# Expert weights loaded once into the first halves of two attention buffers, their row statistics taken on ScalarE, and the last retention units reordered

## Chip, core and metric

The kernel runs on one core of a Trainium2 chip. TensorE (PE) multiplies matrices, VectorE (DVE) and ScalarE (ACT) work on tiles of 128 partitions, GpSimd (POOL) does small arithmetic and indirect DMAs, SyncE (SP) issues most DMAs. The metric is the device time of one execution in microseconds (us). The profile is one such execution taken by the hardware profiler. The granted clock of TensorE stands in it as a share of 2.4 GHz: 1.00 is 2.4 GHz, 0.50 is 1.2 GHz.

## What is computed

The input x holds four sequences of 512 tokens with 128 channels. Four blocks are added to it, one after another: two retention layers with a feed-forward part and a final layer norm, a mixture of experts, causal attention, and the same mixture of experts again. Cut to its core:

```
x = x + retention_layers(layernorm(x))    # 2 layers, 16 heads, decay; FFN 128->512->128 with gelu; ends in layernorm(.., lnf_g, lnf_b)
x = x + moe(layernorm(x))                 # below
x = x + attention(layernorm(x))           # causal, 16 heads of 8, + bo
x = x + moe(layernorm(x))

def moe(x):                               # 2048 tokens, 8 experts, the best 2 of each token
    w, i = top_k(softmax(x @ gate_w), 2); w = w / w.sum(-1)
    return sum over experts e of  (silu(x @ w1[e]) * (x @ w3[e])) @ w2[e]  * (weight of e)
```

The expert weights w1 and w3 are 8 x 2 matrices of 128 x 512 in float32. The kernel multiplies with them as a sum of two float16 parts, high and low, scaled by a power of two for each expert; for the scale it needs a bound on the largest weight of the expert.

## The kernel before

The program has one instruction stream for each engine, written by hand; semaphores tie them together, and every engine takes its stream in order. It has four stages: `blocks()` (the retention layers), `experts(0)`, `attention()`, `experts(1)`.

`blocks()` runs over 8 units (n; two layers times four sequences) of four token tiles each, thus 32 steps t = 4n + u, and two more steps to drain. In step t PE does `keys_values(t)` (L1872), `scores(t)` (L1883), `project_out(t-2)` (L1919), `retain(t-1)` (L1900, L1905, L1909), and, by the position u in the unit, two of the feed-forward's up projections of unit n-2 (L1925; u = 0, 1), the queries and keys of the next unit (L1808; u = 2), or the down projection (L1934) and the transposition for the next feed-forward (`plain_turn(*ln_up(n-1))`, L1797; u = 3). DVE opens each step with the addition of the key and value bias (L985), then multiplies the scores with the decay (L1000, twice), adds outputs, and gates (L1011). ACT copies what PE leaves in the two ring banks of PSUM and does the activations; which use of the banks follows which is fixed in `ring_plan()`.

Into this loop the preparation of the expert weights is woven. `stage` is two halves of the tile X, which held the input. After the four norms of x have been taken, SP loads the experts one after another into the two halves (`expert_in`, L590 to L602), and in steps 7 to 14 DVE takes the largest absolute value of each row (`largest_weight`, L955). The eight columns go to DRAM and come back to every partition (`largest_weights`), and `weight_scales` (L958 to L968) makes the scales in step 17. Then all experts are loaded a second time. In steps 18 to 25 ACT writes the high part (`high_weight`, L1584) and DVE the low part (`low_weight`, L973). A half is loaded again only when both have read it. Afterwards x is loaded again into X (`x_back`), POOL adds the bias of the last norm to it (`add_shift`, L762), and DVE's `leave(s)` adds the retention result of sequence s and takes its sums.

`leave(0)` stands in step 30 on DVE. After the loop PE does `route(0, 0)` (transposition and router logits of sequence 0) and the rest of the last units, while DVE runs `leave_and_route()`: `leave(1)`, `route(0, 0)`, `leave(2)`, `choose_slots(0, 0)` and so on. POOL makes the factors of the norms (`norm_factors`, L712 to L721) and then scatters the rows of tokens to `rows_dram`, 32 indirect DMAs (L775).

`pad_rows` (L613) fills `rows_dram` with 8.4 MB of padding. Expert 7's high part waits for it, because the padding's source lies in its place in `wall`.

`experts(m)` runs over 39 tiles of 128 rows. For tile n SP loads the w2 of its expert into one of three buffers (`w2_load`, L632) and five tiles ahead the rows (`rows_in`, L625); PE does the transposition (L1978), the two up projections (L1989) and `down` (L1999).

`qst` and `kst` are the two attention stacks, each with two halves. The second halves serve other uses during the loop; the first halves hold only rows 72 to 95, constants (zeros in one, three rows of ones in the other). They are written in the first microseconds from `fills` (L551) and copied to the second halves later (`stack_again`, L662 and L664).

## Time and profile before

| what | us |
|---|---|
| median of 3 runs (lowest, highest) | 889.42 (888.31, 891.47) |
| profiled execution | 889.34 |
| its span, first to last instruction | 887.3 |
| PE busy, share of the span | 654.9, 74% |
| DVE busy | 609.1, 69% |
| ACT busy | 354.8, 40% |
| POOL busy | 294.6, 33% |
| mean granted clock of TensorE | 0.866 |

The stages follow each other on all engines. The loop of the blocks lasts from about 20 to 280 us, routing with its scatters to 351 us, the first expert pass starts on PE at 354.65 us. In the first 22 us the SP queue issues the inputs one behind another, and at 21.73 us the padding. A line of a timeline gives start and duration of a group of like instructions, and in brackets how long the engine had waited before it and for whom. "issue" in brackets is a wait whose releaser the profile does not show. Line numbers are those of the kernel before.

### The profile page before, as it was taken

To read this page: it belongs to the slowest core of one execution; us is meant where nothing else is said; L and a number is where in the kernel's file an instruction comes from. 1 tells how busy PE (TensorE), PEld (TensorE's weight loads), DVE (VectorE), ACT (ScalarE), POOL (GpSimd) and SP (SyncE) were. 2 spreads that over 40 slices of the span, in tenths; PEclk is the share of its full clock that TensorE was granted. 3 is DMA by queue.
4 is the path that set the end of the run, shared out by engine and by line. 5 is a ranking of instruction groups with operands and counts; after the bars stand their busy time and mean duration, and the time that the engine had idled before them with its cause. 6 is when DMAs were issued, how large, how long until landed. Compare 5 with 4: busy or idle time off the path is not lost.

```text
span 887.3 us, 19344 instructions
## 1 busy us (share of the span) xinstructions
PE 654.9 (74%) x6492; PEld 453.9 (51%) x6492; DVE 609.1 (69%) x1789; ACT 354.8 (40%) x605; POOL 294.6 (33%) x602
## 2 busy tenths in 40 slices
PE   2758998667868520999935788898898982499990
PEld 1434654435536420999933234444444442399990
DVE  2687876554686883688855677678678735387874
ACT  3204555453533420444414045555564561244440
POOL 1113344141433575355530201110512222355551
PEclk9788999987998855899976589999999995699995
DMA  9995211121100031556533512221312000265554
GB/s 229 193 184 120 96 49 48 48 66 31 49 19 2 3 81 46 146 165 171 167 120 101 130 30 56 76 57 46 101 40 67 15 14 18 81 171 152 167 146 148
DMA packets 102265, 81.00 MB, mean 91 GB/s; under 512 B 8380, under 2 KB 92412, under 8 KB 101980
## 3 DMA queue, kind: packets, MB, share of 16 engines
q1 hardware_dynamic: 96568, 68.35, 31.9%
q0 software_dynamic: 4544, 9.38, 3.1%
q10 hardware_dynamic: 1056, 2.04, 0.6%
q8 instruction: 54, 0.88, 0.4%
q14 instruction: 43, 0.35, 0.1%
HBM read 54.56 MB, written 23.20 MB: 88 GB/s over the span
## 4 chain that ended last, share of the span: by engine, by line
PE 55%; DVE 16%; issue 10%; DMA 6%; POOL 6%; ACT 4%; SPq 2%; ACTq 0%; DVEq 0%; POOLq 0%
PE PC L1999 8%; PE PA L1989 5%; PE PB L1989 5%; DVE rmax L1374 4%; POOL rows_dram L775 4%; PE PC L1905 4%; PE P L2077 4%; PE PA L2037 3%; PE PA L1883 3%; PE PA L2035 3%; PE P L1934 3%; PE P L1925 2%; PE P L1808 2%; DMA ffn_w<-in_w 2%; PE PC L2060 2%
## 5 line engine op out<-in xcount | busy, mean ns | idle before, releaser
L1374 DVE TENSOR_REDUCE rmax<-PA 128x1 f32<-128x512 f32 (+3 forms) x256 | 120.0, 489 | 50.1 <-PE PA L2037 43.3
L787 POOL DMA_INDIRECT outs_dram<-va,ids x78 | 81.2, 1041 | 94.4 <-DVE va L1313 89.9
L1999 PE MATMUL PC<-ffn_w,pm 128*128 128x128 f32 x624 | 87.0, 283 | 3.2 <-DMA ffn_w<-in_w 3.1
L775 POOL DMA_INDIRECT rows_dram<-va,idx x64 | 63.2, 988 | 77.9 <-DVE va L1242 59.1
L2037 PE MATMUL PA<-kst,qst 96*128 96x512 bf16 (+3 forms) x256 | 83.7, 332 | 0.0
L2035 PE MATMUL PA<-mqb,idb 128*128 128x128 bf16 x256 | 60.3, 237 | 24.7 <-DVE rmax L1374 17.4
L1999 PEld LDWEIGHTS PC<-ffn_w,pm 128*128 128x128 f32 x624 | 75.8, 192 | 4.6 <-DMA ffn_w<-in_w 3.9
L1641 ACT ACTIVATE kv_b<-P 128x256 f16<-128x256 f16 x78 | 29.9, 383 | 116.2 <-PE P L1978 116.2
L1303 DVE SCALAR_TENSOR_TENSOR pm<-PB,invb,decay 128x512 f32<-128x512 f32 x78 | 58.5, 750 | 19.5 <-ACT decay L1649 12.8
L2035 PEld LDWEIGHTS PA<-mqb,idb 128*128 128x128 bf16 x256 | 25.3, 99 | 86.9 <-DVE rmax L1374 47.6
L1989 PE MATMUL PA<-kv_b,pm 128*128 128x128 f16 x936 | 66.9, 223 | 0.0
L752 POOL COPY va<-vs 128x128 f32<-128x128 f32 x32 | 10.1, 315 | 171.2 <-DVE vs L985 171.2
L1989 PE MATMUL PB<-kv_b,pm 128*128 128x128 f16 x936 | 66.3, 222 | 0.0
L1649 ACT ACTIVATE decay<-PA,invb 128x512 f32<-128x512 f32 x78 | 53.6, 687 | 28.0 <-PE PA L1989 27.9
L1734 ACT ACTIVATE pm<-PB 128x1024 f32<-128x1024 f32 (+1 forms) x64 | 45.0, 702 | 49.5 <-PE PB L2060 49.3
L1989 PEld LDWEIGHTS PA<-kv_b,pm 128*128 128x128 f16 x936 | 57.5, 100 | 0.0
L1989 PEld LDWEIGHTS PB<-kv_b,pm 128*128 128x128 f16 x936 | 56.8, 99 | 0.0
L1734 ACT ACTIVATE pm<-PC 128x1024 f32<-128x1024 f32 (+1 forms) x64 | 44.9, 702 | 26.5 <-PE PC L2060 26.3
L1294 DVE COPY pm<-wall 128x2048 f16 x78 | 54.2, 695 | 0.3 <-issue 0.3
L1978 PE MATMUL P<-state,proj_w 128*128 128x128 f16 x156 | 22.1, 225 | 40.0 <-DMA proj_w<-rows_dram 22.9
L1797 PE MATMUL P<-const,xn 128*128 128x128 f32 x92 | 17.6, 325 | 42.7 <-ACT xn L1593 30.7
L2077 PE MATMUL P<-pm,va 128*32 128x128 f32 (+3 forms) x512 | 48.2, 449 | 0.0
(239 smaller groups left out, 1472.7 us busy)
## 6 DMA issues: line engine op xcount, KB each, us to landing
ffn_w<-in_w SPq DMA_DIRECT2D x78, 256.0 KB
rows_dram<-wall SPq DMA_DIRECT2D x1, 8385.0 KB, 54.0
X<-in_w SPq DMA_DIRECT2D x32, 256.0 KB, 2.9
proj_w<-rows_dram SPq DMA_DIRECT2D x78, 65.0 KB, 2.0
qst<-parts_dram SPq DMA_DIRECT2D x48, 96.0 KB
kst<-parts_dram SPq DMA_DIRECT2D x48, 96.0 KB
parts_dram<-qkp SPq DMA_DIRECT2D x16, 256.0 KB, 2.7
R<-outs_dram SPq DMA_DIRECT2D x4, 512.0 KB, 3.8
```

What stands on the lines that cost most here:

```text
L775: nc.gpsimd.indirect_dma_start(out=rows_dram, out_offset=bass.IndirectOffsetOnAxis(ap=idx[:, t, r:r + 1], axis=0), in_=xrow[:, t, :], in_o ...
L787: nc.gpsimd.indirect_dma_start(out=outs_dram, out_offset=bass.IndirectOffsetOnAxis(ap=ids[:, k % YB:k % YB + 1], axis=0), in_=ysb[:, k % Y ...
L1294: nc.vector.tensor_copy(wbuf[:, k % 2, :, :, :].rearrange("p i w n -> p (i w n)").unsqueeze(1), wall[:, bass.ds(e, 1), :, :, :].rearrange( ...
L1303: nc.vector.scalar_tensor_tensor(out=eT[:, k % 2, :, :].rearrange("p f n -> p (f n)"), in0=PB[:, k % 2, :], scalar=invb[:, k % 2:k % 2 + 1 ...
L1374: nc.vector.tensor_reduce(rmax[:, i, h % HG:h % HG + 1], PA[:, n % 2, 0:(i + 1) * P], AX_X, ALU.max).then_inc(pair_sb[n % 2], 1)
L1649: nc.scalar.activation(silu_a[:, k % 2, :], PA[:, k % 2, :], ACT.Silu, scale=invb[:, k % 2:k % 2 + 1]).then_inc(m1_si, 1)
L1734: nc.scalar.activation(pt[:, u % 4, :, 0:w], (PB, PC)[u % 2][:, :, 0:w], ACT.Exp, scale=SCALE).then_inc(ex_sb, 1)
L1989: ins = mm(bank[:, k % 2, f * P:(f + 1) * P], wbuf[:, k % 2, part, w, f * P:(f + 1) * P], x16[:, k % 2, x * P:(x + 1) * P], start=i == 0, ...
L1999: ins = mm(PC[:, k % 2, 0:D], eT[:, k % 2, f, :], w2b[k % WB2][:, f, :], start=f == 0, stop=f == FB - 1)
L2035: mm(bank[:, i * P:w], idb[:, :], mqb[:, :], start=True, stop=False, skip_group_check=True)
L2037: mm(bank[:, 0:w], qst[0:KS, s % 2, o + i * P:o + w], kst[0:KS, s % 2, o:o + w], start=False, stop=True, skip_group_check=True).then_inc(p ...
L2077: ins = mm((P6, P7)[b][32 * a:32 * a + 32, j * P:L], vq[:, j, b, g, a, :], pt[:, u % 4, k, 0:(TPS - j) * P], start=j == 0 and g == 0, stop ...
```

## The change

All eight experts are loaded at the start, once, each into a place of its own in the first halves of the two stacks (`stage[e]`). In steps 4 to 7 of the loop ACT takes, instead of the maximum, the sum of the absolute values of each row, two experts a step (`weight_sum`, an activation with an accumulated output). The scales are made in step 9, the high parts on ACT in steps 10 to 17, the low parts on DVE in steps 12 to 19. x is never overwritten, so it is not loaded again; `add_shift` goes into steps 11, 15, 19 and 23. The padding is issued behind the scales' DMAs. `leave(0)` stands in step 29; the transposition and the router of sequence 0 stand in the two draining steps. The constant rows of all four stack halves, and bo, are written by SP between two w2 loads of the first expert pass. The rows to scatter in the first pass and some small tables of sequence 0 lie in other places.

The diff, cut:

```diff
+SUMS_AT, SCALE_AT, HIGH_AT, LOW_AT = 4, 9, 10, 12
...
         if n >= 2:
-            plan += [("up", n - 2, f) for f in range(FB)]
+            plan += [("up", n - 2, 0), ("up", n - 2, 1)]
+        if n == UNITS:
+            plan += [("turn", LNM1, 0)]
+        if n >= 2:
+            plan += [("up", n - 2, 2), ("up", n - 2, 3)]
+        if n == UNITS:
+            plan += [("router", 0, 0)]
...
-        stage = tuple(X[:, 8 * b:8 * b + 8, :].rearrange("p t n -> p (t n)") for b in range(2))
+        raw = tuple(stack[:, 0, :].bitcast(F32) for stack in (qst, kst))
+        stage = tuple(raw[2 * e // E][:, e % (E // 2) * 2 * F:(e % (E // 2) + 1) * 2 * F] for e in range(E))
+        all_sums = wall32[:, 0:2 * F]
+        xrow0 = raw[0][:, 0:NT * XROW].rearrange("p (t c) -> p t c", t=NT)
...
-            sp.wait_ge(filled, 2)
-            for stack, fill in ((qst, zeros), (kst, ones)):
-                sp.dma_start(stack[KQ:KS, 0, :].rearrange("r (h n) -> r h n", h=H),
-                             fill.unsqueeze(1).to_broadcast([KS - KQ, H, L])).then_inc(stack_fill, 16)
...
+            for e in range(E):
+                sp.dma_start(stage[e][:, 0:F], a_w1[e]).then_inc(stage_in[e], 16)
+                sp.dma_start(stage[e][:, F:2 * F], a_w3[e]).then_inc(stage_in[e], 16)
...
                     w2_load(n, expert[n])
+                    if (m, n) == (0, 2):
+                        stack_constants()
+                        sp.dma_start(bo[:, :], a_bo.partition_broadcast(P)).then_inc(in_att, 16)
...
+            def stack_constants():
+
+                sp.wait_ge(filled, 3)
+                for b in range(2):
+                    for stack, fill in ((qst, zeros), (kst, ones)):
+                        sp.dma_start(stack[KQ:KS, b, :].rearrange("r (h n) -> r h n", h=H),
+                                     fill.unsqueeze(1).to_broadcast([KS - KQ, H, L])).then_inc(stack_fill, 16)
+
+            largest_weights()
             pad_rows()
-            for e in range(2 * E):
-                expert_in(e)
-                if e == E - 1:
-                    largest_weights()
             sp.wait_ge(w_hi, E)
             sp.wait_ge(w_lo, E)
-            for s in range(SEQ):
-                sp.dma_start(X[:, TPS * s:TPS * s + TPS, :], x_t[:, TPS * s:TPS * s + TPS, :]).then_inc(x_back[s], 16)
...
-                    if n == UNITS - 1:
-                        add_shift(0)
+                if u == 3 and 2 <= n < SEQ + 2:
+                    add_shift(n - 2)
+                if t == LAST - 1:
+                    norm_factors(STAT[(LNM1, 0)])
...
-                    if E - 1 <= t < 2 * E - 1:
-                        largest_weight(t - E + 1)
-                    if t == 2 * E + 1:
+                    if t == SCALE_AT:
                         weight_scales()
-                    if 2 * E + 2 <= t < 3 * E + 2:
-                        low_weight(t - 2 * E - 2)
-                    if t == LAST - 2:
+                    if LOW_AT <= t < LOW_AT + E:
+                        low_weight(t - LOW_AT)
+                    if t == LAST - 3:
                         leave(0)
...
+            def weight_sum(e):
+
+                act.wait_ge(stage_in[e], 32)
+                if e >= 2:
+                    act.wait_ge(w_max, e - 1)
+                nc.scalar.activation(wall32[:, (1 + e % 2) * 2 * F:(2 + e % 2) * 2 * F], stage[e], ACT.Abs,
+                                     accum_out=amax[:, e:e + 1]).then_inc(w_max, 1)
...
                 def weights(t):
-                    if 2 * E + 2 <= t < 3 * E + 2:
-                        high_weight(t - 2 * E - 2)
+                    if SUMS_AT <= t < SUMS_AT + E // 2:
+                        weight_sum(2 * (t - SUMS_AT))
+                        weight_sum(2 * (t - SUMS_AT) + 1)
+                    if HIGH_AT <= t < HIGH_AT + E:
+                        high_weight(t - HIGH_AT)
...
+                    if t == LAST:
+                        plain_turn(LNM1, 0)
+                    if t == LAST + 1:
+                        router(0, 0).then_inc(ring_ps, 1)
...
-                route(0, 0)
                 down(UNITS - 2)
```

ACT, steps 5 to 8, before. The rows are line, operation, written tile <- read tiles, shape and count; `xT` is a transposed tile, `kst` the queries, `qkf`/`qkp` the queries and keys, `xn` the normalized rows, `va` the gate input.

```order
L1599 ACTIVATE va<-P,proj_bc 128x512
L1497 ACTIVATE xT<-P,lnb,lng 128x512
L1505 ACTIVATE kst<-P,proj_bq,const 128x512 x4
L1507 ACTIVATE qkf<-P,proj_bc 128x512
L1510 ACTIVATE qkp<-P,proj_bc 128x512
L1593 ACTIVATE xn<-R,nrm 128x128 x4
L1497 ACTIVATE xT<-P,lnb,lng 128x512
L1599 ACTIVATE va<-P,proj_bc 128x512
```

The same place after the change.

```order
L1604 ACTIVATE va<-P,proj_bc 128x512
L1581 ACTIVATE wall,amax<-qst 128x1024 x4
L1491 ACTIVATE xT<-P,lnb,lng 128x512
L1499 ACTIVATE kst<-P,proj_bq,const 128x512 x4
L1501 ACTIVATE qkf<-P,proj_bc 128x512
L1504 ACTIVATE qkp<-P,proj_bc 128x512
L1581 ACTIVATE wall,amax<-kst 128x1024 x2
L1598 ACTIVATE xn<-R,nrm 128x128 x4
L1491 ACTIVATE xT<-P,lnb,lng 128x512
L1581 ACTIVATE wall,amax<-kst 128x1024 x2
L1604 ACTIVATE va<-P,proj_bc 128x512
```

The eight sums (L1581) stand in three places: four ahead of a transposed tile, two directly ahead of the normalization, two behind the next transposed tile.

SP in the first expert pass, before: from the third w2 load (`ffn_w<-in_w`) to the fourth. TENSOR_LOAD and ISA rows read the expert's number and the row.

```order
L632 DMA ffn_w<-in_w 128x4x128
L622 TENSOR_LOAD dst
L622 ISA x2
L625 ISA
L625 DMA proj_w<-rows_dram 128x130
L632 ISA
L632 DMA ffn_w<-in_w 128x4x128
```

The same place after the change.

```order
L626 DMA ffn_w<-in_w 128x4x128
L654 DMA qst<-vs 24x16x512
L654 DMA kst<-vs 24x16x512
L654 DMA qst<-vs 24x16x512
L654 DMA kst<-vs 24x16x512
L636 DMA bo<-in_bo 128x128
L616 TENSOR_LOAD dst
L616 ISA x2
L619 ISA
L619 DMA proj_w<-rows_dram 128x130
L626 ISA
L626 DMA ffn_w<-in_w 128x4x128
```

Five DMAs now stand between the third and the fourth w2 load.

## Rows read from the trace of the kernel before

**Rows 1.** Windows: busy of PE, PEld, DVE, ACT, POOL; granted clock, DMA share, GB/s.

```profile
80.00:100.00 20.00, 19.52 (x175) 10.57 (x176) 18.02 (x38) 9.05 (x13) 8.62 (x26) 1.00 0.27 88
...
200.00:220.00 20.00, 16.52 (x116) 10.83 (x106) 8.68 (x22) 7.47 (x8) 1.98 (x3) 0.76 0.10 28
```

**Rows 2.** Groups of lines, 0 to 300 us: busy, mean ns | idle before, releaser.

```profile
L973 DVE SCALAR_TENSOR_TENSOR wall<-X,wscale,wall 128x1024 f16<-128x1024 f32 x8 | 11.1, 1387 | 33.1 <-ACT wall L1584 33.1
...
L955 DVE TENSOR_REDUCE amax<-X 128x1 f32<-128x1024 f32 x8 | 9.6, 1205 | 0.0
L1584 ACT ACTIVATE wall<-X,wscale 128x1024 f16<-128x1024 f32 x8 | 9.2, 1145 | 0.0
```

**Rows 3.** Timeline of DVE: start, duration, line, names, [idle before <-releaser].

```profile
82.97 0.41 DVE L985 TENSOR_TENSOR vs<-PC,kv_b 128x256 f32<-128x256 f32 x1
...
106.23 0.42 DVE L985 TENSOR_TENSOR vs<-PC,kv_b 128x256 f32<-128x256 f32 x1 [0.61 <-PE PC L1872]
...
132.69 0.42 DVE L985 TENSOR_TENSOR vs<-PC,kv_b 128x256 f32<-128x256 f32 x1 [1.74 <-PE PC L1872]
...
143.52 2.01 DVE L961 TENSOR_REDUCE amax<-X 128x8 f32<-128x1024 f32 x1
...
208.09 1.28 DVE L973 SCALAR_TENSOR_TENSOR wall<-X,wscale,wall 128x1024 f16<-128x1024 f32 x1 [6.15 <-ACT wall L1584]
...
243.27 0.42 DVE L985 TENSOR_TENSOR vs<-PC,kv_b 128x256 f32<-128x256 f32 x1 [1.74 <-PE PC L1872]
...
278.31 0.29 DVE L1036 TENSOR_TENSOR R<-PC,R 128x128 f32<-128x128 f32 x1 [1.81 <-PE PC L1919]
...
294.16 1.19 DVE L889 SCALAR_TENSOR_TENSOR rs<-rs 128x4 f32<-128x4 f32 x1
...
298.03 0.16 DVE L891 SCALAR_TENSOR_TENSOR rs<-rs 128x4 f32<-128x4 f32 x1
```

**Rows 4.** Timeline of POOL, 290 to 310 us.

```profile
295.28 2.50 POOL L762 TENSOR_TENSOR X<-X,lnf 128x512 f32<-128x512 f32 x2
...
308.24 1.19 POOL L775 DMA_INDIRECT rows_dram<-va,idx  x1 [0.65 <-issue]
```

**Rows 5.** DMA issues, 0 to 360 us: count, KB each, us to landing.

```profile
rows_dram<-wall SPq DMA_DIRECT2D x1, 8385.0 KB, 54.0
X<-in_w SPq DMA_DIRECT2D x32, 256.0 KB, 2.9
...
X<-amax_dram SPq DMA_DIRECT2D x1, 512.0 KB, 3.8
```

**Rows 6.** Timeline of ACT.

```profile
71.33 0.78 ACT L1497 ACTIVATE xT<-P,lnb,lng 128x512 f32<-128x512 f32 x1 [20.93 <-PE P L1797]
...
78.59 1.65 ACT L1593 ACTIVATE xn<-R,nrm 128x128 f32<-128x128 f32 x4
```

**Rows 7.** Timeline of PE.

```profile
80.39 0.63 PE L1797 MATMUL P<-const,xn 128*128 128x128 f32 x4 [1.21 <-ACT xn L1593]
...
146.93 0.46 PE L1919 MATMUL PC<-reto_w,vs 128*128 128x128 f32 x2 [1.83 <-issue]
...
147.98 1.67 PE L1905 MATMUL PC<-pm,va 128*32 128x128 f32 x32
...
172.24 1.08 PE L1905 MATMUL PC<-pm,va 128*32 128x128 f32 x32
...
266.30 0.77 PE L1919 MATMUL PC<-reto_w,vs 128*128 128x128 f32 x2 [6.75 <-issue]
...
368.67 1.11 PE L1999 MATMUL PC<-ffn_w,pm 128*128 128x128 f32 x8
```

**Rows 8.** Timeline of SP's queue.

```profile
363.93 0.38 SPq L632 DMA_DIRECT2D ffn_w<-in_w  x1
```

**Rows 9.** Windows of 1 us, columns as in the first group.

```profile
261.00:262.00 1.00, 0.00 (x0) 0.00 (x0) 0.83 (x6) 1.00 (x3) 0.00 (x0) 1.00 1.01 197
```

**Rows 10.** DMA issues between 69 and 71 us.

```profile
X<-in_w SPq DMA_DIRECT2D x4, 256.0 KB, 6.8
```

121 lines of the change are left out of this document (52 added, 69 removed).

## Prediction, made before the changed kernel ran

> **What bounds the kernel now.** I read the windows, the groups of lines and the timelines, in this order. The windows show the granted clock of TensorE: between 80 and 100 us it is 1.00 (2.4 GHz) and PE is busy 19.5 of 20 us, between 200 and 220 us it is 0.76, with PE at 16.5 and VectorE (DVE) at only 8.7 of 20 us [rows 1]. So the 32-step loop of the retention stage has a dense part and a slack part. The groups of lines name the slack: the eight `low_weight` instructions (L973) work 11.1 us and are preceded by 33.1 us in which DVE waits for ScalarE's (ACT) `high_weight` (L1584) [rows 2]. DVE takes its work in order, so PE waits behind it.
>
> The timeline of DVE gives the price. One `keys_values` addition (L985) opens each step: step 8 at 82.97, 12 at 106.23, 16 at 132.69, 28 at 243.27 [rows 3]. Steps 12 to 15 take 26.46 us; steps 16 to 27 take 110.58 us, against 3 x 26.46 = 79.38 at the pace of the unit before. The missing 31.2 us are the eight waits, the scale computation at step 17, and what PE loses at half clock after its pauses. The row at 208.09 shows one wait, 6.15 us: ACT had its operand late, because the expert's load may only start when the staging half is free again.
>
> The next part is routing: 32 row scatters on GpSimd (POOL), the first at 308.24 [rows 4], then two expert passes and attention. The change touches routing and the first expert pass only slightly.
>
> **The waits on high weights.** All eight experts now lie in SBUF before the loop needs them. The 16 loads are 4 MB; a 256 KB load takes 2.9 us from issue to landing [rows 5], and they stand in the SP queue behind the inputs, where the pad write had stood, thus from about 20 us. Even one after another that is 46 us, thus 66 us for the last. The first four sums are placed in ACT's idle stretch, 20.93 us long and ending at 71.33 [rows 6], so they cost nothing. Each `high_weight` then stands on ACT two steps ahead of its `low_weight` on DVE, and waits for no load. I cost the waits at nothing: two steps are 13 us, the copy is 1.145 us [rows 2]. The DVE work of 1.39 us per step takes the room of the removed maximum (1.205 us), which had stood in steps 7 to 14 of the dense part, where PE was busy 19.5 of 20 us. For the same reason the removed maxima give no time: PE is the bound there. So steps 12 to 27 should run at the pace of 26.46 per unit.
>
> **The sums on ACT.** Steps 4 and 5 are covered as said. The pair of step 6 stands directly before the normalization at 78.59 (L1593), and PE already waits 1.21 us for that one at 80.39 [rows 6, 7]. Two sums of about 1.145 us (the nearest row is the 128x1024 ACT copy) put 2.3 us on the path. PE's pause there grows to 3.5 us. Whether it then drops to 1.2 GHz I cannot tell: after 1.83 us of waiting the 32-matmul group L1905 ran 1.67 us, where one at 2.4 GHz takes 1.08 [rows 7]. Bounds 0 and 1.7 us; I take 1.7, since even a shorter pause was followed by it. The pair of step 7 lies in waiting time of the same size. Step 8 opens at 82.97 + 4.0 = 87.0. An accumulator read could add a few tenths.
>
> DVE's maximum takes 1205 ns and the ACT copy of the same tile 1145 ns [rows 2]. The Trainium skill, page "ScalarE: Activation LUTs", section "Rules for kernel authors", says that such plain operations belong on VectorE; by that rule the sums should have stayed, and the time would be 4.0 us lower than my forecast, since the trace shows DVE's maxima hidden under PE. The same page's section "What ACT_TABLE_LOAD costs" gives 186 ns + 0.833 ns per element, an estimate of 1.04 us a sum.
>
> **The scales.** `weight_scales` moves from step 17 to step 9. It takes 2.9 us, 2.01 of them one reduction [rows 3]. At step 17 it cost PE a pause of 1.83 us and the slow group after it [rows 7]; I charge 1.8 + 1.6 = 3.4 us at step 9, which replaces the same cost inside the 110.58 us. Its operand: the last sum ends near 88.5, then come a small write, two issues and the broadcast read, which took 3.8 us to land [rows 5], so it is there at about 94.5; DVE gets to it at about 96. It does not wait, but with only 1 to 2 us to spare.
>
> **Sum of the loop.** Step 12 opens at 87.0 + 23.26 + 3.4 = 113.7, step 28 at 113.7 + 4 x 26.46 = 219.5, against 243.27: 23.8 us earlier.
>
> **The pad rows.** The 8.4 MB write moves from 21.73 us to behind the scales' DMAs, about 94 us; it took 54.0 us with other loads in front of it [rows 5], so it lands by 148. Expert 7's `high_weight` waits for it with step 17; step 16 opens at 113.7 + 26.46 = 140.2 and half a unit later ACT is there, at about 151. Hidden, with 3 us of margin.
>
> **The end of the loop.** `leave(0)` stands one step earlier. It stopped PE for 6.75 us [rows 7]; its 7 us of DVE work stop PE again, so I give this 0 to 1.4 us, take 0.6 (less PE work is then left behind the pause). The earlier turn and router of sequence 0 move ACT and PE work away from a place where DVE sets the end; they gain nothing and put one PE transposition ahead of the result that DVE waits for at 278.31, included in the 0.6. POOL's two additions of the shift, 295.28 to 297.78, stretched two 0.16 us DVE instructions to 1.2 us each (the row at 294.16 is one such, the row at 298.03 one without an addition beside it) [rows 3, 4]. These two additions move into the loop: 2 x 1.03 = 2.1 us. Together 2.7 us, which the first scatter passes on, as it starts when POOL has sequence 2's factors. In the loop the same additions fall on a DVE with waiting time.
>
> **The constant rows of the stacks.** Four DMAs of 384 KB now go on the SP queue between the third and the fourth load of w2, with bo behind them. PE has three w2 buffers and a tile lasts 2.4 us (down(3) at 368.67, its load issued at 363.93 [rows 7, 8]). The load took about 3 us, so there is 1.5 us to spare. A 384 KB copy between the two halves of a stack moved 197 GB/s [rows 9], 2.0 us; four are 8 us, and 10 us if the 16-way source broadcast is slower. Do loads wait behind an earlier transfer of their queue? The four loads issued at 69 us, while the pad write was still running, landed after 6.8 us instead of 2.9 [rows 5, 10]. So yes. The fourth w2 load lands near 376.5 instead of 367.5; PE stops for 6.8 to 8.8 us, I take 7.8, and with the half clock afterwards (1.8) this costs **9.6 us**. Nothing gives it back, since PE sets the pace of the tiles. This stall is new: POOL, DVE and ACT queue behind it too.
>
> The Trainium skill, page "DMA: Bandwidth & Descriptors", section "Queues, rings and completion order", says that each DMA engine takes descriptors of one ring in order, yet that completion is not first-in first-out per issuing engine. By the first half the stall stands, by the second a load could come past, and the time would be 862.8.
>
> **Sum.** 23.8 + 2.7 - 9.6 = 16.9 us. The profiled execution before took 889.34 us (span 887.3), the median of the three runs 889.42; both agree. 889.4 - 16.9 = **872.5**.
>
> **Rivals.**
> - *The w2 loads come past the constant rows, or the fill is short* (862.8). For it: 24 rows hardly fill all engines. Against it: the 6.8 us landing. 0.22.
> - *The hidden parts are not hidden* (876 to 882). The amax path is 2 us late and stops DVE at step 9, the pad ends a few us late at step 17, or a sum takes 1.4 us; each is priced at 2 to 5 us. The margins are 1 to 3 us. 0.20.
> - *The waits only move* (900): ACT still reaches `high_weight` after DVE wants the result. Then the 23.8 us turn into a loss of 4.0 (the sums), with 9.6 lost and 2.7 gained: 889.4 + 4.0 + 9.6 - 2.7 = 900.3. Against it: two steps of lead on an engine that is busy 9 of 20 us. 0.04.
> - *The pad write holds ACT* (slower from one point on): if it lands 17 us or more after 151 us, thus 74 us after its issue, `high_weight(7)` keeps the gelus of that unit from PE and the gain is eaten; at half the former rate it lands at 202 and the time is 923. Against it: nothing else loads then. 0.02.
>
> **How the numbers follow.** The forecast has 0.49, 0.03 lies around no change. Faster by over 0.3% (about what a measurement can tell) means below 886.8: 0.49 + 0.22 + 0.20 = 0.91; same 0.03; slower 0.06. The range is 861 to 882: the lower end is the first rival with the clock loss of 1.7 not paid, the upper one the second rival.
>
> **What would show it.** In the profile after: L973's successor waits about 0 for ACT; steps 12 to 28 at 26.5 us a unit; PE's clock 1.00 from 100 to 210 us; a PE wait for `ffn_w` of 7 to 8 us at the fourth down projection; 3.5 us before the first turn of ln_up; DVE's inverse roots at 0.16 us all through. The forecast is wrong if the granted clock in the dense part is below 1.00, or if a unit takes 30 us.

## The result, and the profile after

The changed kernel takes 877.98 us (median of 4 runs, 876.51 to 879.05), the kernel before, in the same comparison, 889.63 us (median of 4 runs, 888.31 to 891.47): a ratio of 0.9865 with a 95% interval from 0.9844 to 0.9887. That is 11.65 us gained where the prediction had 16.9, so 877.98 against 872.5 us. It lies in the range, and most of the terms were near. One execution below, the fourth of low_away, took 1296.36 us against 875 to 879 us in the other three, and is left out of the median given there. The main point is another: the experiments show that the largest term was explained by the wrong cause, and that one number in the kernel before gives more than the whole change.

"Step t" is the t-th step of the loop, and it opens with the addition of `keys_values` on DVE. These are windows of the kernel after; the columns are those of [rows 1], and so are the first two stretches. The other two are the first expert pass:

```profile
80.00:100.00 20.00, 15.16 (x119) 7.58 (x120) 13.72 (x32) 10.60 (x19) 4.35 (x8) 0.91 0.59 122
200.00:220.00 20.00, 18.96 (x193) 12.46 (x191) 12.37 (x32) 10.17 (x20) 9.79 (x39) 1.00 0.01 2
331.00:345.00 14.00, 13.02 (x156) 12.54 (x156) 7.64 (x19) 6.92 (x12) 3.41 (x6) 0.78 0.56 139
345.00:357.00 12.00, 2.54 (x15) 2.48 (x16) 1.29 (x4) 0.21 (x1) 0.86 (x2) 0.60 0.73 168
```

The slack part of the loop is dense now (PE 18.96 of 20 us at clock 1.00, before 16.52 at 0.76), the dense part has a hole (15.16 instead of 19.52 us between 80 and 100), and in the expert pass there are 12 us in which PE works 2.54. The groups of lines that answer to [rows 2], of the first 300 us:

```profile
L968 DVE SCALAR_TENSOR_TENSOR wall<-kst,wscale,wall 128x1024 f16<-128x1024 f32 x4 | 5.1, 1267 | 0.0
L968 DVE SCALAR_TENSOR_TENSOR wall<-qst,wscale,wall 128x1024 f16<-128x1024 f32 x4 | 5.1, 1266 | 0.0
```

These are the eight low parts. Ahead of them DVE waits 0.0 us; before it was 33.1. The rows that answer to [rows 3], [rows 4] and [rows 7], each from the timeline of its engine (start, duration, what, idle before and releaser):

```profile
84.37 0.42 DVE L980 TENSOR_TENSOR vs<-PC,kv_b 128x256 f32<-128x256 f32 x1 [1.64 <-PE PC L1884]
...
91.95 0.42 DVE L980 TENSOR_TENSOR vs<-PC,kv_b 128x256 f32<-128x256 f32 x1 [1.77 <-PE PC L1884]
...
96.48 1.99 DVE L956 TENSOR_REDUCE amax<-wall 128x8 f32<-128x1024 f32 x1
...
99.09 0.42 DVE L980 TENSOR_TENSOR vs<-PC,kv_b 128x256 f32<-128x256 f32 x1
...
111.94 0.42 DVE L980 TENSOR_TENSOR vs<-PC,kv_b 128x256 f32<-128x256 f32 x1 [1.50 <-PE PC L1884]
```

```profile
83.28 0.63 PE L1808 MATMUL P<-const,xn 128*128 128x128 f32 x4 [3.29 <-ACT xn L1598]
...
99.62 0.46 PE L1931 MATMUL PC<-reto_w,vs 128*128 128x128 f32 x2 [1.56 <-issue]
...
100.67 1.08 PE L1917 MATMUL PC<-pm,va 128*32 128x128 f32 x32
...
238.76 0.77 PE L1931 MATMUL PC<-reto_w,vs 128*128 128x128 f32 x2 [5.95 <-issue]
...
354.46 2.07 PE L2014 MATMUL PC<-ffn_w,pm 128*128 128x128 f32 x8 [9.75 <-DMA ffn_w<-in_w]
```

```profile
283.04 1.19 POOL L776 DMA_INDIRECT rows_dram<-qst,idx  x1 [0.21 <-issue]
...
305.15 0.96 POOL L776 DMA_INDIRECT rows_dram<-qst,idx  x1 [1.56 <-DVE qst L1236]
...
325.24 0.95 POOL L776 DMA_INDIRECT rows_dram<-qst,idx  x1 [0.30 <-issue]
```

Where the time went, read from the timelines of both kernels (us from the span's start; the gain is the difference of the starts, the last column what the stretch up to there added):

| point | before | after | gain | of this stretch |
|---|---|---|---|---|
| step 12 opens | 106.23 | 111.94 | -5.7 | -5.7 |
| step 28 opens | 243.27 | 220.41 | 22.9 | +28.6 |
| first scatter | 308.24 | 283.04 | 25.2 | +2.3 |
| first product of the first expert pass | 354.65 | 330.98 | 23.7 | -1.5 |
| last down product of that pass | 450.26 | 437.42 | 12.8 | -10.8 |
| end of the span | 887.3 | 875.6 | 11.7 | -1.1 |

The pass itself, from the first product to the last down product, takes 95.61 us before and 106.44 after.

### The profile page after: what moved, and what is told of

Read it like the earlier page. It is cut to its first block, busy times and chain, and to the rows that moved or that the text cites. A ratio compares the mean times of both kernels' runs of the same rounds, so it can differ in the third digit from the quotient of the medians.

```text
span 875.6 us, 19336 instructions
## 1 busy us (share of the span) xinstructions
PE 651.0 (74%) x6492; PEld 447.7 (51%) x6492; DVE 598.8 (68%) x1783; ACT 363.4 (42%) x621; POOL 298.9 (34%) x602
## 4 chain that ended last, share of the span: by engine, by line
PE 35%; DVE 13%; DMA 6%; issue 5%; SPq 4%; POOL 3%; ACT 2%; ACTq 0%; DVEq 0%; POOLq 0%
PE PC L2014 7%; PE PA L2004 5%; DVE rmax L1368 5%; PE PB L2004 5%; PE P L2092 4%; PE PA L2052 3%; PE PA L2050 3%; POOL rows_dram L776 3%; DMA ffn_w<-in_w 2%; PE PC L2075 2%; PE PB L2075 1%; DVE X L1315 1%; SPq L616 1%; DMA R<-outs_dram 1%; PE PA L2059 1%
## 5 line engine op out<-in xcount | busy, mean ns | idle before, releaser
L2014 PE MATMUL PC<-ffn_w,pm 128*128 128x128 f32 x624 | 87.8, 284 | 12.7 <-DMA ffn_w<-in_w 12.6
L2050 PEld LDWEIGHTS PA<-mqb,idb 128*128 128x128 bf16 x256 | 25.2, 98 | 87.4 <-DVE rmax L1368 48.1
L776 POOL DMA_INDIRECT rows_dram<-va,idx x32 | 31.4, 980 | 69.3 <-DVE va L1236 60.6
## 6 DMA issues: line engine op xcount, KB each, us to landing
rows_dram<-wall SPq DMA_DIRECT2D x1, 8385.0 KB, 52.5
```

What stands on the lines that cost most here:

```text
L776: nc.gpsimd.indirect_dma_start(out=rows_dram, out_offset=bass.IndirectOffsetOnAxis(ap=idx[:, t, r:r + 1], axis=0), in_=xrow_[m][:, t, :], ...
L2014: ins = mm(PC[:, k % 2, 0:D], eT[:, k % 2, f, :], w2b[k % WB2][:, f, :], start=f == 0, stop=f == FB - 1)
L2050: mm(bank[:, i * P:w], idb[:, :], mqb[:, :], start=True, stop=False, skip_group_check=True)
```

## Experiments on the first expert pass

The prediction's second large term was a loss: four row fills of 384 KB and `bo` stand in SP's queue ahead of the fourth load of w2. The queue of SP in the kernel after shows them:

```profile
338.24 0.38 SPq L626 DMA_DIRECT2D ffn_w<-in_w  x1
338.67 1.03 SPq L654 DMA_DIRECT2D qst<-vs  x1
339.76 0.78 SPq L654 DMA_DIRECT2D kst<-vs  x1
340.58 2.23 SPq L654 DMA_DIRECT2D qst<-vs  x1
342.85 2.21 SPq L654 DMA_DIRECT2D kst<-vs  x1
345.11 2.30 SPq L636 DMA_DIRECT2D bo<-in_bo  x1
...
349.56 1.91 SPq L626 DMA_DIRECT2D ffn_w<-in_w  x1
```

w2's next load is issued 11.3 us behind the one before, lands at 354.4, and PE starts at 354.46 after 9.75 us of waiting, at half clock (2.07 us for a group that takes 1.11 us [rows 7]).

**fills_out**: three fills go under the scattering of the rows, the fourth and `bo` behind the last w2 load.

```diff
             sp.dma_start(wo, a_wo).then_inc(in_att, 16)
+            stack_constants([(0, kst, ones), (1, qst, zeros), (1, kst, ones)])
             experts(0)
...
-                    if (m, n) == (0, 2):
-                        stack_constants()
+                    if (m, n) == (0, NTL - 1):
+                        stack_constants([(0, qst, zeros)])
                         sp.dma_start(bo[:, :], a_bo.partition_broadcast(P)).then_inc(in_att, 16)
```

> Against the changed kernel (878.0 us) only the place of the five constant transfers differs: three of the four row fills are issued right behind wo (at 298 us of the trace, under the scattering of the rows), the last one and bo behind the last w2 load of the first expert pass. Theory A (they stood in front of a w2 load in one queue): w2 load 4 is issued near 339 instead of 349.6, TensorE's wait of 9.75 us at the fourth tile's down product falls under 1 us, and of the 10.2 us that the stretch from the first tile to the attention's first scores lost, 8 to 10 come back: 868 to 870 us. Theory B (the fills cost the same wherever they stand, since they fill the DMA engines): the last scatter or the landing of the rows comes 4 to 8 us later, 872 to 876 us. Theory C (the wait has another cause, such as w2's own transfers): the 9.75 us stay, 878 us.

Measured: 864.41 us (863.15 to 866.81), ratio to before 0.9709 (0.9668 to 0.9750). The first pass takes 95.68 us, as in the kernel before. The scatters, beside which three of the fills now run, take 41.56 us from the first to the last, against 42.20 in the changed kernel and 40.3 to 42.2 in all kernels without fills there. So the whole of the 10.8 us came back, and nothing that can be seen was paid for it elsewhere: Theory A, not B or C. The profiled span is 10.6 us shorter; the median is 13.6 us lower and lies below Theory A's 868 to 870. In the seven kernels with the block at its old place the pass takes 106.2 to 108.2 us, so the price of the block varies between 10.6 and 12.6 us from one execution to the next, and the changed kernel's trace shows it near its lowest.

```profile
345.00:357.00 12.00, 12.00 (x174) 11.94 (x171) 10.31 (x26) 5.37 (x11) 6.66 (x10) 1.00 0.58 166
```

The same 12 us as in the window above, now with PE busy throughout, at clock 1.00.

But this does not say what it was about the old place. Two more kernels do, which keep the fills in the pass, one a tile.

**fills_spread**: one of the five transfers behind each of the w2 loads 3 to 7, in SP's queue.

```diff
-                    if (m, n) == (0, 2):
-                        stack_constants()
+                    if m == 0 and 2 <= n < 6:
+                        stack_constants([(0, qst, zeros), (0, kst, ones), (1, qst, zeros), (1, kst, ones)][n - 2:n - 1])
+                    if (m, n) == (0, 6):
                         sp.dma_start(bo[:, :], a_bo.partition_broadcast(P)).then_inc(in_att, 16)
```

> The same five transfers stay in SP's queue of the first expert pass, but one stands behind each of the w2 loads 3 to 7 instead of all five behind load 3. Theory A (each costs about 2.2 us of the queue, as SP's issue times of 2.2 to 2.3 us show, and a tile of 2.40 us leaves the queue some slack): the 9.75 us wait splits into waits of at most 2 us at five tiles, in sum 4 to 6 us, 872 to 874 us. Theory B (only the length of the block counts and what is spread is hidden): under 1.5 us of waits, 868 to 870 us. Theory C (the sum of the transfers' time counts, spread or not): 9 to 10 us of waits, 878 us.

Measured: 875.11 us (874.07 to 875.63), ratio 0.9833 (0.9793 to 0.9872). The pass takes 103.69 us, 8.1 more than before: three waits of 3.39, 1.40 and 0.20 us for w2, and half clock behind them. Spreading won 2.7 of 10.8 us. The waits sum to 5.0 us, as Theory A has it (4 to 6), but one is longer than its 2 us, and with the half clock the pass loses more: the median lies between A's 872 to 874 us and C's 878.

**fills_act**: the same five, one behind the gate of each of the tiles 2 to 6, issued by ACT on its own queue.

```diff
                     gate(k)
+                    if 2 <= k < 6:
+                        act.wait_ge(filled, 3)
+                        b, stack, fill = [(0, qst, zeros), (0, kst, ones), (1, qst, zeros), (1, kst, ones)][k - 2]
+                        act.dma_start(stack[KQ:KS, b, :].rearrange("r (h n) -> r h n", h=H),
+                                      fill.unsqueeze(1).to_broadcast([KS - KQ, H, L])).then_inc(stack_fill, 16)
+                    if k == 6:
+                        act.dma_start(bo[:, :], a_bo.partition_broadcast(P)).then_inc(in_att, 16)
```

> The same transfers, one a tile as in fills_spread, but issued by ScalarE (its own queue) behind the gate of tiles 2 to 6. Theory A (it was the place ahead of the w2 loads in one queue): w2 loads are issued on time, the down product's wait falls under 1 us, 868 to 870 us. Theory B (it was the DMA engines' time, whichever queue carries it): w2 loads land late by as much as in fills_spread, 872 to 874 us or what fills_spread gives. Theory C (the issuing engine is held 2.2 us by each issue, as SP was): ScalarE holds the gates of five tiles, TensorE waits for ScalarE 1 to 2 us at each, 874 to 880 us.

Measured: 873.22 us (872.44 to 875.65), ratio 0.9822 (0.9781 to 0.9863). The pass takes 105.37 us, 9.8 more than before, although nothing stands ahead of w2 in SP's queue. PE waits for w2 as before, in pieces:

```profile
344.43 1.16 PE L2011 MATMUL PC<-ffn_w,pm 128*128 128x128 f32 x8 [1.94 <-DMA ffn_w<-in_w]
...
351.00 1.93 PE L2011 MATMUL PC<-ffn_w,pm 128*128 128x128 f32 x8 [3.96 <-DMA ffn_w<-in_w]
...
356.29 1.16 PE L2011 MATMUL PC<-ffn_w,pm 128*128 128x128 f32 x8 [1.05 <-DMA ffn_w<-in_w]
```

and the window of the same stretch shows the DMA engines full (share 0.97, 188 GB/s):

```profile
345.00:357.00 12.00, 6.99 (x72) 6.56 (x71) 4.07 (x10) 2.14 (x4) 2.65 (x4) 0.86 0.97 188
```

So Theory A falls, and B holds for this kernel, with the median in its 872 to 874 us: the w2 loads are issued with nothing ahead of them and still land late (the fifth, issued at 340.99 us, only at 351.0, when PE starts). Theory C is not seen, since the issue of a fill holds ACT for only 0.8 to 1.4 us and PE does not wait for it. The pass needs 166 GB/s for its own loads, a share of 0.58 (fills_out, 345 to 357 us); four fills of 384 KB are 1.57 MB on top, by an estimate 8.4 us at 188 GB/s, and the loads have little to spare: in fills_out the first down product waits 0.43 us for w2. The Trainium skill, page "DMA: Bandwidth & Descriptors", section "Issuing engines are not separate DMA queues", states this: transfers of whatever engine run on the same 16 DMA engines, and several issuers save only issue time. The trace agrees: 9.8 us on ACT's queue, 8.1 and 10.8 us on SP's.

This does not make the queue innocent in the changed kernel. There the share was only 0.73 in the same window, and the fourth w2 load was issued at 349.56 us, where fills_out issued it at 340.29: SP had been held by its own issues, up to 2.3 us each. What the runs show is that either way costs about the same. In one queue the load waits for its issue; in two it is issued in time and lands late. How the 10.8 us of the changed kernel divide between the two was not measured.

## Experiments on the loop

**sums_early**: all eight row sums at steps 4 and 5.

```diff
-                    if SUMS_AT <= t < SUMS_AT + E // 2:
-                        weight_sum(2 * (t - SUMS_AT))
-                        weight_sum(2 * (t - SUMS_AT) + 1)
+                    if SUMS_AT <= t < SUMS_AT + 2:
+                        for e in range(4):
+                            weight_sum(4 * (t - SUMS_AT) + e)
```

> The eight row sums stand four at step 4 and four at step 5 of ScalarE's order, instead of two at each of steps 4 to 7; all raw weights have landed by 30 us, and ScalarE waits 17.0 us for TensorE from 55 to 72. Theory A (the sums of steps 6 and 7 hold the turn of the second sequence, as the prediction has it, 2.3 us and 1.7 us of clock): TensorE's wait of 3.29 us ahead of that turn falls to about 1.2 us, step 8 opens at 82 to 83 instead of 84.4 us, and 2 to 4 us come back: 874 to 876 us. Theory B (what the sums hold is made up again by the next wait, that for the scales at step 9, since amax then only comes earlier and DVE is the bound of the steps): under 1 us, 877 to 878 us.

Measured: 871.88 us (868.75 to 875.12), ratio 0.9804 (0.9753 to 0.9855). From step 7 to step 12 the loop takes 31.42 us instead of 35.06, so 3.6 us come back; the wait ahead of the turn is down to the 1.21 us of [rows 7]:

```profile
78.86 0.63 PE L1808 MATMUL P<-const,xn 128*128 128x128 f32 x4 [1.21 <-ACT xn L1598]
```

Theory A in cause and size; the median is 6.1 us lower, below its range. The other 2.5 us are not shown to be the edit's: step 6 opens between 67.1 and 70.0 us in kernels whose sums are alike, and step 4, ahead of the edit, already opened 1.4 us earlier here.

Then the main term. The prediction explained the 33.1 us of waiting so: ACT's operand was late, since a load may only start when a staging half is free again. The change does two things at these instructions, however. It keeps all eight experts in SBUF, and it puts the high part (ACT) two steps ahead of the low part (DVE), where both stood in the same step. Four kernels take them apart.

**reload_free**: every expert is loaded a second time, without a wait for a buffer.

```diff
             largest_weights()
+            for e in range(E):
+                sp.wait_ge(w_max, e + 1)
+                sp.dma_start(stage[e][:, 0:F], a_w1[e]).then_inc(stage_in[e], 16)
+                sp.dma_start(stage[e][:, F:2 * F], a_w3[e]).then_inc(stage_in[e], 16)
             pad_rows()
...
                 act.wait_ge(w_scaled, 1)
+                act.wait_ge(stage_in[e], 64)
```

The pad rows lie in a tail of `work` that is free here, so expert 7's high part does not wait for them, in this kernel and the next.

> The changed kernel, but every expert's raw w1 and w3 are loaded a second time into their own place, as soon as the sums have been taken and sent (from about 95 us), and the high part of an expert waits for its second copy; the pad rows' transfer stands behind them, from a place of its own. It puts back the 4 MB of traffic that the change removed, but not the wait for a free buffer. Theory A (the loop's gain comes from the waits for a free buffer, not from the traffic): the second copies land at 385 GB/s from 95 to about 106 us, each ahead of its use at steps 10 to 17; step 28 opens at 220 to 222 us, total 877 to 880 us. Theory B (the traffic itself slowed the steps of before): 4 to 10 us slower, 882 to 888 us.  A first copy that lands after step 10 opens (97 to 99 us) would cost 1 to 3 us once, and lies within A.

Measured: 877.08 us (876.47 to 877.43), ratio 0.9859 (0.9833 to 0.9885), step 28 at 221.12 us. Theory A: the 4 MB of traffic that the change removed cost nothing that can be seen.

**reload_gated**: the second load of expert e also waits until the low part of expert e - 2 is done, as with two buffers.

```diff
             for e in range(E):
                 sp.wait_ge(w_max, e + 1)
+                if e >= 2:
+                    sp.wait_ge(w_lo, e - 1)
```

> As reload_free, but the second copy of expert e (from e = 2) is only asked for once the low part of expert e - 2 is done, as in the kernel before with its two buffers; sums, scales, high and low parts stay at the changed kernel's steps. Theory A (the 33.1 us in which VectorE waited for the high part, because its raw weights had only begun to load when a buffer came free, are what the loop gained): VectorE waits again ahead of the low part at steps 14 to 19, 3 to 6 us each and 20 to 30 us in sum; step 28 opens at 240 to 245 us, total 896 to 903 us. Theory B (the gain came from elsewhere, such as the reductions that left VectorE): under 8 us slower than reload_free, 880 to 886 us.

Measured: 887.09 us (882.36 to 890.31), ratio 0.9967 (0.9946 to 0.9988). Step 28 opens at 227.83 us. The waits for the loads are there, but on ACT, 15.0 us in sum (groups of lines, 80 to 262 us):

```profile
L1594 ACT ACTIVATE wall<-kst,wscale 128x1024 f16<-128x1024 f32 x4 | 4.6, 1154 | 8.4 <-DMA kst<-in_w 8.4
L1594 ACT ACTIVATE wall<-qst,wscale 128x1024 f16<-128x1024 f32 x4 | 4.6, 1152 | 6.6 <-DMA qst<-in_w 6.6
```

and DVE waits 0.0 us ahead of its low parts. The loop is 7.4 us longer than in the changed kernel, the median 9.1 us. Neither theory had that: A had asked for 896 to 903 us, and B's bound of 8 us over reload_free was passed by 2. The waits for a free buffer are real, and worth about a third of what I had put on them.

**high_same**: all experts resident, but the high part back in the step of the low part.

```diff
-SUMS_AT, SCALE_AT, HIGH_AT, LOW_AT = 4, 9, 10, 12
+SUMS_AT, SCALE_AT, HIGH_AT, LOW_AT = 4, 9, 12, 12
```

> The changed kernel with all eight experts resident as before, but the high part of an expert on ScalarE stands in the same step as its low part on VectorE (both from step 12), as it did in the kernel before, instead of two steps ahead. Theory A (what made VectorE wait 33.1 us is that ScalarE comes to the high part only behind the step's turn, queries and keys, after VectorE wants it; the lead of two steps took that away, not the residency): VectorE waits 15 to 33 us ahead of its low parts, step 28 opens 10 to 24 us later than at 220.4, total 888 to 902 us. Theory B (residency took the waits away, as the prediction has it with the load that starts only when a staging half is free): the copies are there, so the waits stay under 4 us in sum, total 878 to 882 us.

Measured: 904.68 us (899.90 to 905.47), ratio 1.0159 (1.0132 to 1.0185): 15.8 us slower than the kernel before, whose median beside it was 888.86. Step 28 opens at 246.92 us. The waits are back to the last us (groups of lines, 100 to 262 us), with every weight in place since 30 us:

```profile
L968 DVE SCALAR_TENSOR_TENSOR wall<-kst,wscale,wall 128x1024 f16<-128x1024 f32 x4 | 6.0, 1492 | 17.1 <-ACT wall L1589 17.1
...
L968 DVE SCALAR_TENSOR_TENSOR wall<-qst,wscale,wall 128x1024 f16<-128x1024 f32 x4 | 5.1, 1285 | 16.9 <-ACT wall L1589 16.9
```

**before_lead**: the kernel before, two buffers and all, with the low part two steps later.

```diff
-                    if 2 * E + 2 <= t < 3 * E + 2:
-                        low_weight(t - 2 * E - 2)
+                    if 2 * E + 4 <= t < 3 * E + 4:
+                        low_weight(t - 2 * E - 4)
```

> The kernel before with one number changed: the low part of expert e on VectorE stands at step 20 + e instead of 18 + e, so two steps behind its high part; two staging buffers, two loads and all else as before. Theory A (the lead is what counts; the wait for a free buffer costs what reload_gated lost, about 7 to 9 us): VectorE's 33.1 us of waits fall to under 10 us, step 28 opens at 225 to 235 instead of 243.3 us, total 873 to 882 us, so near the changed kernel without any weight being resident. Theory B (with two buffers the loads set the pace whatever the order): the waits move to ScalarE and hold it instead, step 28 at 240 to 245, total 886 to 891 us.

Measured: 872.37 us (869.59 to 872.55), ratio 0.9801 (0.9784 to 0.9818). Step 28 opens at 226.20 us, and DVE waits 0.0 us ahead of L973. This number alone beats the changed kernel by 5.6 us. The loads are now what the high part waits for, 15.2 us in sum, where it waited for none in the kernel before (groups of lines, 80 to 280 us):

```profile
L1584 ACT ACTIVATE wall<-X,wscale 128x1024 f16<-128x1024 f32 x8 | 9.2, 1149 | 15.2 <-DMA X<-in_w 15.2
```

So late operands are in this kernel and not in the kernel before, and yet it is the faster one.

| | low part in the high part's step | low part two steps later |
|---|---|---|
| two buffers, reloaded | before: step 28 at 243.27; 889.63 | before_lead: 226.20; 872.37 |
| the same in the changed kernel | not run | reload_gated: 227.83; 887.09 |
| all eight resident | high_same: 246.92; 904.68 | changed kernel: 220.41; 877.98 |

Read across, two steps are worth 17.1 us at step 28 without residency and 26.5 us with it. Read down, residency is worth 7.4 us with the lead and nothing without it: steps 12 to 28 take 137.13 us in high_same and 137.04 in the kernel before, although the scales are made within them only in the latter. (The totals of the changed kernel's rows hold the 10.8 us of the fills as well.)

The mechanism can be seen in high_same, on ACT and on DVE:

```profile
115.67 0.69 ACT L1608 ACTIVATE qst<-P,ffn_b 128x512 f32<-128x512 f32 x1 [0.17 <-PE P L1937]
116.25 1.14 ACT L1589 ACTIVATE wall<-qst,wscale 128x1024 f16<-128x1024 f32 x1
123.53 0.69 ACT L1608 ACTIVATE qst<-P,ffn_b 128x512 f32<-128x512 f32 x1 [6.14 <-PE P L1937]
124.39 0.69 ACT L1608 ACTIVATE qst<-P,ffn_b 128x512 f32<-128x512 f32 x1 [0.17 <-PE P L1937]
124.97 1.14 ACT L1589 ACTIVATE wall<-qst,wscale 128x1024 f16<-128x1024 f32 x1
```

```profile
117.42 1.29 DVE L968 SCALAR_TENSOR_TENSOR wall<-qst,wscale,wall 128x1024 f16<-128x1024 f32 x1 [1.90 <-ACT wall L1589]
...
126.14 1.28 DVE L968 SCALAR_TENSOR_TENSOR wall<-qst,wscale,wall 128x1024 f16<-128x1024 f32 x1 [3.42 <-ACT wall L1589]
```

ACT gets to the high part at 124.97 because two gelus stand ahead of it, and these wait for PE (6.14 us). PE does its up projections behind the retention, and comes to that only at 119.15, after a pause of 2.02 us, when DVE has made the addition of 118.63 (L980); this stands on DVE behind the low part, which waits for the high part. It is a ring of three engines, in which no one is short of data. The kernel before does the same at its steps of the same kind: the waits there are 1.90 us at 177.03 and 3.35 us at 185.72.

**low_away**: the low parts at steps in which POOL computes no normalization factors.

```diff
-                    if LOW_AT <= t < LOW_AT + E:
-                        low_weight(t - LOW_AT)
+                    if t in (12, 15, 16, 19, 20, 23, 24, 27):
+                        low_weight((12, 15, 16, 19, 20, 23, 24, 27).index(t))
```

In the changed kernel one small operation in each of POOL's chains at steps 13, 14, 17 and 18 is stretched beside a low part, for example:

```profile
150.10 0.20 POOL L719 TENSOR_TENSOR nrm<-nrm 128x4 f32<-128x4 f32 x1
150.38 1.25 POOL L716 TENSOR_TENSOR nrm<-nrm 128x4 f32<-128x4 f32 x1
```

```profile
150.29 1.27 DVE L968 SCALAR_TENSOR_TENSOR wall<-kst,wscale,wall 128x1024 f16<-128x1024 f32 x1
```

> The eight low parts stand at steps 12, 15, 16, 19, 20, 23, 24 and 27 instead of 12 to 19, so that none runs in a step in which GpSimd computes normalization factors (13, 14, 17, 18, 21, 22). In the trace a 128x4 operation of GpSimd that takes 0.20 us elsewhere took 1.25 us at 150.38 and at 158.41, each while VectorE ran a low part. Theory A (the low part holds GpSimd's chain, and at step 18 that chain holds ScalarE and TensorE): no such long operation in the chains, TensorE's wait of 2.4 us ahead of the turn at step 18 falls under 1 us, the stretch from step 12 to step 28 (108.5 us) gets 2 to 3.5 us shorter: 874.5 to 876 us. Theory B (VectorE is the bound in every step, and 1.27 us a step is paid wherever it stands): within 1 us, 877 to 879 us.

Measured: 877.58 us (874.95 to 878.90, three runs), ratio 0.9873 (0.9839 to 0.9907). In the trace no operation of these chains takes over 0.9 us any more, and PE's wait ahead of the turn at step 18 is 1.58 instead of 2.42 us. Steps 12 to 28 take 107.59 us, but what to compare this with is uncertain: 108.47 in the changed kernel, 109.8 in fills_out, sums_early, shift_late and best, 111.3 to 111.4 in fills_act, fills_spread and reload_free, all with the low parts at the same steps. The median shows nothing of it (Theory B's 877 to 879). So the stretching is real; what it costs the loop is 0.9 to 3.8 us by these traces, and that any of it reaches the end is not shown.

One reason why such stretches differ can be seen in low_away itself. PE pauses 1.58 us ahead of two turns, and the same group of 32 matmuls behind it runs once at full clock and once at a little over half:

```profile
150.84 0.63 PE L1808 MATMUL P<-const,xn 128*128 128x128 f32 x4 [1.58 <-ACT xn L1598]
...
151.67 1.08 PE L1917 MATMUL PC<-pm,va 128*32 128x128 f32 x32
...
177.38 0.82 PE L1808 MATMUL P<-const,xn 128*128 128x128 f32 x4 [1.58 <-ACT xn L1598]
...
178.56 1.94 PE L1917 MATMUL PC<-pm,va 128*32 128x128 f32 x32
```

The unit with the first takes 26.55 us, the unit with the second 28.06.

**shift_late**: POOL's additions of the shift back at their old places.

```diff
-                if u == 3 and 2 <= n < SEQ + 2:
-                    add_shift(n - 2)
...
             add_ffn2(UNITS - 2)
+            add_shift(1)
...
             add_ffn2(UNITS - 1)
+            add_shift(2)
+            add_shift(3)
```

(and `add_shift(0)` at step 28)

> GpSimd adds lnf's shift to x at the places of the kernel before (one at step 28, one behind the last unit's bias, two together behind the last bias) instead of at steps 11, 15, 19 and 23. Theory A (in the loop it is hidden, since GpSimd waits about 5 us for VectorE's keys and values behind it, and at the end it stretches VectorE's 128x4 operations to 1.2 us each): steps 8 to 28 as in the changed kernel within 1 us, two or three such long operations of VectorE ahead of the first scatter, which comes 1 to 3 us later; 879 to 881 us. Theory B (in the loop it holds the factors of steps 13 and 17 and so the units of 27.5 and 29.1 us): the loop gets 2 to 3 us shorter, 875 to 878 us in sum.

Measured: 877.98 us (876.81 to 880.95), ratio 0.9881 (0.9851 to 0.9912). From step 28 to the first scatter it takes 64.3 us, against 61.5 to 62.6 in the changed kernel and the ten others that have the additions in the loop, and 64.9 in before_lead, which has them late as well. The reason is on DVE: three operations of 0.16 us are stretched to 1.2, one beside POOL's addition of a bias (L726) and two beside its additions of the shift (L763). The one beside the bias is there in the changed kernel too (1.19 us at 271.37).

```profile
269.42 1.20 DVE L892 SCALAR_TENSOR_TENSOR rs<-rs 128x4 f32<-128x4 f32 x1
270.65 1.19 DVE L894 SCALAR_TENSOR_TENSOR rs<-rs 128x4 f32<-128x4 f32 x1
271.87 1.19 DVE L891 TENSOR_TENSOR rs<-rs 128x4 f32<-128x4 f32 x1
```

```profile
269.33 1.26 POOL L726 TENSOR_TENSOR R<-R,ffn_b 128x512 f32<-128x512 f32 x1
270.56 2.49 POOL L763 TENSOR_TENSOR X<-X,lnf 128x512 f32<-128x512 f32 x2
```

Theory A for the place and the size in the trace; the median lies below its 879 to 881 and is the changed kernel's own. The loop from step 8 to 28 takes 137.2 us here, and 136.0 to 138.8 us in the five kernels that differ from this one in the loop only by the additions or by a second load, so they are hidden there. A gain of about 2 us is too small for the medians.

**best** and **best2**: the fills of fills_out, the sums of sums_early and one more edit; best2 adds low_away's steps.

```diff
                 leave(1)
-                route(0, 0)
                 add_ffn(UNITS - 2)
+                route(0, 0)
                 leave(2)
```

> The changed kernel with three edits: the row fills placed as in fills_out, the sums as in sums_early, and VectorE's addition for unit 6 ahead of the first routing instead of behind it, since TensorE stood idle for 6.92 us until that addition (at 268.73) freed its bank. If the parts add up: 878.0 less 10.8 (the first pass of fills_out against the changed kernel), less 3.6 (steps 7 to 12 in sums_early), less 0 to 1.5: 862 to 864 by the changed kernel's median; by fills_out's own median (864.4) 859 to 861. The third edit by itself: TensorE's wait ahead of the up product falls from 6.9 to about 4 us; the first scatter does not move, because it stands behind GpSimd's factors of sequence 2 (until 282.8), but the wait of 1.6 us in the chain of scatters goes; a rival is that it moves nothing, since VectorE is the bound from 255 to 304 us.

> As best, and the low parts at steps 12, 15, 16, 19, 20, 23, 24 and 27 as in low_away, whose trace had steps 12 to 28 in 107.6 us (108.5 to 109.8 us in the others) but whose median did not show it. If the 1 to 2 us are real, this is 1 to 2 us below best; if GpSimd's stretched operations cost nothing on the path that sets the end, the two are alike within 1 us.

Measured: best 861.65 us (859.12 to 864.15), ratio to before 0.9683 (0.9664 to 0.9702), just below the 862 to 864 expected from the changed kernel's median; best2 859.25 us (857.11 to 863.51), ratio 0.9662 (0.9646 to 0.9678). Both beat both kernels; 2.4 us between them with overlapping intervals, and spans of 862.2 and 861.7, do not tell them apart. The third edit shortened PE's wait ahead of the up product from 6.92 to 4.33 us, and the wait in the chain of scatters (1.56 us) is gone, but first to last scatter takes 41.18 us against 41.56 in fills_out: it moved nothing that can be seen. The sum of the parts holds for the pass (95.34 us) and the loop. But the attention stage, in which nothing was edited, took 241.7 us in best, 241.4 in best2 and 240.8 in low_away, and 236.6 to 239.8 us in all others (238.3 in the changed kernel); why is open. It may be the reason that best's median is only 2.8 us below fills_out's, where the sums alone gave 3.6 in the loop.

What I did not run: before_lead with anything of the change on top. Its loop ends 5.8 us later than the changed kernel's, and it has no stall in the pass.

## Why the prediction was right or wrong

*The waits on the high weights: the size was right, the cause was wrong.* They went to 0.0, and step 28 opened 22.9 us earlier, predicted 23.8. The step that failed is the sentence "ACT had its operand late, because the expert's load may only start when the staging half is free again". high_same has the operands in place and waits 34.0 us; before_lead has them late and waits 0.0. It could have been read in [rows 2]: L1584, the high part, has 0.0 us of idle time of its own, so it never waited for a load; ACT merely got to it late, behind work that waited for PE. The prediction did name the two steps of lead, but as an addition to residency; and its rival "the waits only move", with a chance of 0.04, has the true cause in half a sentence ("ACT still reaches `high_weight` after DVE wants the result"). That the gain came out all the same is luck: the change held both the supposed cure and the real one. One sum should have warned: the 31.2 us that steps 16 to 27 had too many were to hold the eight waits, the scales and the lost clock, but the waits alone are 33.1, so some of them stand where DVE would have waited for PE (1.74 us in the row at 132.69).

*The waits at nothing, 26.46 us a unit: too good.* The four units from step 12 to 28 took 27.5, 29.1, 25.9 and 25.9 us, 108.5 in sum instead of 105.8. Once DVE no longer waits, POOL's chains of normalization factors are late next: PE waits 2.42 us ahead of the turns at steps 14 and 18 (127.36 and 154.88 us), and each chain has one operation stretched by the low part beside it. low_away takes the stretching away and 0.9 us of the 2.7, if one trace may be set against another; the rest hangs on where a pause is followed by half clock, which the prediction had at nothing here and which changes from execution to execution.

*The sums on ACT: right in size (4.0 predicted, 3.6 by sums_early), wrong in place.* Step 8 opened only 1.4 us late. The pause ahead of the turn was 3.29 us (predicted 3.5), but the half clock was paid behind it, so step 9 opened 4.2 us late. The sum itself is 1.04 to 1.06 us, which agrees with the 1.04 that the prediction worked out from the Trainium skill ("ScalarE: Activation LUTs", "What ACT_TABLE_LOAD costs"); each has a row of 0.19 to 0.21 us more for reading the accumulator, which overlaps. As to that page's rule that such operations belong on VectorE, the trace does not bear it out here: the 4.0 us were a matter of the step, not of the engine. At steps 4 and 5 the same eight sums on ACT cost nothing.

*The scales at step 9: too dear.* 3.4 us were charged. Step 10 opened 7.14 us after step 9, against 5.64 in the kernel before: 1.5 us. PE paused 1.56 us and the group behind it ran at full clock (1.08 us), where the pause of 1.83 us at step 17 had been followed by 1.67 [rows 7]. The operand did not make DVE wait, as predicted. With the sums, step 12 opened 1.8 us earlier than predicted (111.9, not 113.7); steps 12 to 28 took 2.7 us more than predicted. These two errors cancel all but 0.9 us in the loop's sum, which is luck too.

*The pad rows:* 52.5 us from issue to landing, no wait for them at step 17. Right.

*The end of the loop:* 2.7 us predicted, 2.3 measured at the first scatter. The 5.95 us pause behind `leave(0)` is 0.8 shorter than before (0.6 taken), and shift_late shows two stretched operations where they were expected, at 1.7 to 2.8 us. The prediction took the row at 294.16 for one of these two; it stands beside POOL's bias addition (294.06 to 295.33) and is still there after the change.

*From the first scatter to the first tile: not in the prediction.* It assumed that the chain of 32 scatters passes everything on. 1.5 us were lost there in this trace. DVE delivers sequence 3's rows 1.26 us too late for the chain (the row at 305.15, a wait of 1.56 where 0.30 is usual), and four scatters behind the first take 1.3 instead of 0.96 us, two in the kernel before. But the loss is not fixed: fills_act and fills_spread have the same program up to the pass, and take 46.0 us from the first scatter to the first product, less than the kernel before (46.4) and the changed kernel (47.9); their wait is 0.30.

*The constant rows: 9.6 us predicted, 10.8 measured (a wait of 9.75, predicted 7.8); the mechanism is half of it.* "Do loads wait behind an earlier transfer of their queue? So yes" was drawn from four loads that landed late behind the pad write. In the changed kernel the load did wait behind the fills in SP's queue, for its issue. But fills_act shows about the same loss with two queues, the engines then being full. The row that the prediction drew on fits both readings, since the pad write keeps the DMA engines busy in either; a price from it was safe, and a remedy (another queue, or spreading) would not have been.

*Its own signs.* The granted clock in the dense part, which was to be 1.00 if the forecast held, was 0.91 between 80 and 100 us, from the pause that it had priced itself; between 100 and 210 us it was 0.98. No unit took 30 us in the changed kernel (29.1 the longest), but one took 30.4 in fills_act, fills_spread and reload_free. DVE's inverse roots were not at 0.16 us all through: one took 1.19.

*The rest*, 1.1 us behind the pass, is within what the attention stage varies by from kernel to kernel.

In sum: 0.9 us of the loop, 0.4 of its end, 1.5 in the scatters, 1.2 in the fills and 1.1 behind make the 5.2 us by which the profiled spans missed the forecast (11.7 instead of 16.9).

## What to carry to other kernels

When one engine waits for another, read what stood ahead of the awaited instruction on its own engine: if that was waiting for a third engine, try a lead of a step or two in the program's order first; here neither the buffers nor the earlier loads replaced it. Before a transfer is put into a loop fed by DMA, compare the engines' share of that loop (0.58 here) with the bytes added, and do not count on another queue; under the scattering, where the share was 0.18, the fills were free. And a change of several parts is worth taking apart even when it wins: here one number gave more than all of it. Before a difference of 1 or 2 us between two traces is explained, look at a third one: the same steps 12 to 28 took 108.5 to 111.4 us in seven kernels with the same order there.
